# Tile 0 of a mixture-of-experts layer takes its experts by id, and a part of the weight conversion changes engine and order

## What is computed

```python
# layer 1, one head of 256
q, k = rope(bf16(x @ Wq.T)), rope(bf16(x @ Wk.T))
o = where(causal, exp(q @ k.T / 16), 0).sum(-1)        # one number per row
x1 = layernorm(x + relu(o * fc1_w + fc1_b) @ fc2_w.T + fc2_b)
# layer 2, 12 experts, three routers, the best 3 of 12 of each
C1, C2, C3 = (top3_softmax(x1 @ P_w.T @ U.T) for U in (U1, U2, U3))   # zero elsewhere
h = gelu(sum_e C1[:, e] * (x1 @ W1[e].T))
y = sum_e C2[:, e] * (h @ W2[e].T) + C3 @ b2
out = layernorm(x1 + y)
```

## Time and profile before

| | us |
|---|---|
| median of 3 runs | 280.23 |
| lowest, highest | 279.22, 280.51 |
| the profiled execution | 280.48 |
| its span, first to last instruction | 278.7 |

### The profile page before, as it was taken

One profiled execution on the slowest core, in us unless ns is written; L12 is line 12 of the kernel. 1 busy time (PEld: TensorE's weight loads), 2 busy tenths in 40 slices (PEclk: granted clock), 3 DMA queues, 4 the chain that ended last, 5 costly groups with the idle time before them and its releaser, 6 DMA issues.

```text
span 278.7 us, 6485 instructions
## 1 busy us (share of the span) xinstructions
PE 257.4 (92%) x2016; PEld 191.4 (69%) x2016; DVE 213.2 (77%) x668; ACT 173.9 (62%) x376; POOL 180.2 (65%) x367
## 2 busy tenths in 40 slices
PE   7999999998989985998999999999999999899980
PEld 5445444554436773877789798799798798798960
DVE  0359959859969865688998899899897788766671
ACT  2235975765852730675958957967878858656541
POOL 2640004999989899747885775775775864856551
PEclk9999999999999996899999999999999999999996
DMA  7999994996000000000010101001011010111012
GB/s 226 378 397 372 164 221 72 220 151 84 0 1 2 0 4 0 0 5 17 13 31 22 34 24 39 22 20 42 19 26 35 20 40 19 33 32 38 23 36 61
DMA packets 19546, 20.51 MB, mean 74 GB/s; under 512 B 1643, under 2 KB 18870, under 8 KB 18998
## 3 DMA queue, kind: packets, MB, share of 16 engines
q1 hardware_dynamic: 18518, 19.14, 27.9%
q10 hardware_dynamic: 992, 0.93, 1.2%
HBM read 15.78 MB, written 4.19 MB: 72 GB/s over the span
## 4 chain that ended last, share of the span: by engine, by line
PE 37%; POOL 21%; SPq 16%; ACT 12%; issue 6%; DVE 5%; DMA 1%; POOLq 0%; ACTq 0%; DVEq 0%
PE bank L1117 31%; POOL W L471 7%; POOL wtmp L468 5%; POOL W L470 5%; SPq L371 4%; SPq L376 3%; ACT L705 3%; SPq L393 2%; SPq L380 2%; DVE early L1535 2%; ACT early L726 2%; PE bank L1197 2%; ACT L788 2%; SPq L404 1%; PE bank L995 1%
## 5 line engine op out<-in xcount | busy, mean ns | idle before, releaser
L1117 PE MATMUL bank<-W,early 128*128 (+1 forms) x630 | 77.7, 278 | 6.0 <-DVE early L1535 3.7
L1117 PE MATMUL bank<-W,x1T 128*128 (+1 forms) x630 | 75.9, 273 | 0.5 <-ACT early L837 0.5
L1117 PEld LDWEIGHTS bank<-W,early 128*128 128x128 f16 x630 | 61.9, 100 | 15.8 <-issue 4.2
L1117 PEld LDWEIGHTS bank<-W,x1T 128*128 128x128 f16 x630 | 60.9, 98 | 8.6 <-issue 1.1
L920 PE MATMUL bank<-early,wqk 128*128 128x512 f32 x128 | 60.1, 602 | 1.1 <-DMA early<-in_xT 1.1
L1535 DVE SCALAR_TENSOR_TENSOR early<-bank,Csel,early 128x256 f32<-128x256 f32 x95 | 45.7, 481 | 9.2 <-PE bank L1117 2.7
L591 POOL TENSOR_TENSOR early<-early 128x256 f32<-128x256 f32 x29 | 21.0, 725 | 28.4 <-DVE early L1535 27.1
L920 PEld LDWEIGHTS bank<-early,wqk 128*128 128x128 f32 x128 | 22.4, 190 | 21.8 <-issue 21.2
L661 ACT ACTIVATE qk<-bank 128x512 bf16<-128x512 f32 x32 | 19.0, 595 | 29.1 <-PE bank L920 28.9
L788 ACT ACTIVATE early<-early 128x256 f32<-128x256 f32 x32 | 13.3, 417 | 35.5 <-DVE early L1535 35.4
L1289 DVE TENSOR_TENSOR xturn<-qk,turn 128x2048 bf16<-128x2048 bf16 x16 | 20.4, 1276 | 15.7 <-ACT qk L661 15.7
(11 more groups left out here) (139 smaller groups left out, 451.6 us busy)
## 6 DMA issues: line engine op xcount, KB each, us to landing
early<-in_xT SPq DMA_DIRECT2D x16, 256.0 KB, 7.8
xs<-in_x SPq DMA_DIRECT2D x32, 128.0 KB, 6.8
out<-early SPq DMA_DIRECT2D x32, 128.0 KB
W<-in_w1T SPq DMA_DIRECT2D x1, 2048.0 KB, 12.2
W<-in_w2T SPq DMA_DIRECT2D x1, 2048.0 KB, 12.8
W<-in_w1T SPq DMA_DIRECT2D x1, 1024.0 KB, 7.7
W<-in_w2T SPq DMA_DIRECT2D x1, 1024.0 KB, 14.3
wqk<-in_wqkT ACTq DMA_DIRECT2D x1, 512.0 KB, 3.8
```

The source lines that it names most:

```text
L1117: mm = pe.matmul(where[:, 0:DIM], lhs(hx, c), w, start=(k == 0), stop=(k == 5))
```

## The change

Tile 0 takes three experts by id in both mixtures, as all other tiles do (`experts_of` and `dense_expert` go). All of W2 must then be converted before `second(0)`. Of W2, six experts (5 down to 0) are now on ScalarE and VectorE and six on GpSimd; W1 stays at four and eight. GpSimd's order is written anew: three pieces, `norm_scale(0)`, two pieces, `norm_scale(1)`, three pieces (W1 is complete), the softmax weights, `select_of(0)`, `C3_split(0)`, five pieces of W2, `bias_add(0, 0)`, the sixth. `route_count(0)` moves ahead of `project(7, 2)`. Group 0's mask is made as the other groups' is, with 4 strikes in place of 12. On TensorE the order after the chunks is: first mixtures of tiles 0, 1, 2, 3, then the second ones of 0 and 1.

```diff
-NB = 4
+NB = (4, 6)
+HERE, THERE = NB[0], NE - NB[0]
...
+            seconds = () if i < GT else (0, 1, 2) if i == GT else (i - 2,)
+            order = [(t, 1, j) for t in seconds for j in range(TOPK)]
+            order += [(i, 0, j) for j in range(TOPK)] if i < NT else []
...
+        def here(n):
+            return (0, NB[0] - 1 - n) if n < HERE else (1, NB[1] - 1 - (n - HERE))
+        def there(n):
+            return (0, NB[0] + n) if n < THERE else (1, NB[1] + n - THERE)
...
             def w_piece(n):
-                m, e = n // (NE - NB), NB + n % (NE - NB)
+                m, e = there(n)
...
-                t = slice(max(GT * g, 1), GT * (g + 1))
+                t = slice(GT * g, GT * (g + 1))
...
-            piece = 0
-            for c in range(NCH):
-                for j in range(4):
-                    if (c, j) == (NCH - 1, 1):
-                        continue
-                    if (c, j) == (3, 3):
-                        norm_scale(0)
-                    if (c, j) == (5, 1):
-                        norm_scale(1)
-                    if (c, j) == (6, 1):
-                        chosen_exps(0)
-                        weights_of(0)
-                    if (c, j) == (6, 2):
-                        C3_split(0)
-                        select_of(0)
-                    if c >= 4:
-                        w_piece(piece)
-                        piece += 1
-            bias_add(0, 0)
-            w_piece(piece)
+            for n in range(THERE):
+                if n == 3:
+                    norm_scale(0)
+                if n == 5:
+                    norm_scale(1)
+                w_piece(n)
+            chosen_exps(0)
+            weights_of(0)
+            select_of(0)
+            C3_split(0)
+            for n in range(THERE, 2 * NE - sum(NB)):
+                if n == 2 * NE - sum(NB) - 1:
+                    bias_add(0, 0)
+                w_piece(n)
...
             norm_scale(2)
+            bias_add(0, 1)
             gate_parts(2)
-            bias_add(0, 1)
+            chosen_exps(1)
             row_scale(0)
-            chosen_exps(1)
...
# ScalarE, after the chunks
             begin(0)
+            begin(1)
             exps(NCH - 1, 0)
-            w_high(NB + 2)
+            w_high(HERE + 2)
             exps(NCH - 1, 1)
-            w_high(NB + 3)
+            w_high(HERE + 3)
+            C3T_copy(0)
             gelu(0)
-            C3T_copy(0)
-            begin(1)
+            gelu(1)
+            begin(2)
+            w_high(HERE + 4)
+            bias_copy(0, 0)
             h_high(0)
-            bias_copy(0, 0)
-            gelu(1)
+            gelu(2)
+            w_high(HERE + 5)
+            begin(3)
+            h_high(1)
+            bias_copy(0, 1)
+            gelu(3)
             normed(2, 0)
-            bias_copy(0, 1)
+            exp_route(1)
             x1_high(2, 0)
-            exp_route(1)
             normed(2, 1)
-            h_high(1)
-            begin(2)
-            gelu(2)
-            gate_copy(2)
             final(0)
             h_high(2)
             x1_high(2, 1)
-            begin(3)
-            gelu(3)
+            gate_copy(2)
...
# TensorE, after the chunks
+            load_ids(0)
+            x1_transpose(1, 1)
+            pe.wait_ge(exp_done, SPC * (NCH - 1))
+            pe.wait_ge(w_split, THERE)
+            pe.wait_ge(wlo_done, HERE)
+            routed_first(0, range(0, 2))
+            pe.wait_ge(qk_copied, 4 * NCH)
+            routed_first(0, range(2, TOPK))
+            fc(2, 0)
+            routed_first(1, range(0, 2))
+            pe.wait_ge(gate_copied, 4)
+            scores(NCH - 1, 0)
+            routed_first(1, range(2, TOPK))
+            fc(2, 1)
+            scores(NCH - 1, 1)
             C3_transpose(0)
-            routed_first(1)
+            routed_first(2)
             pe.wait_ge(exp_done, SPC * NCH)
             h_transpose(0)
             bias(0, 0)
             route_logits(1)
+            h_transpose(1)
+            routed_first(3)
             bias(0, 1)
+            pe.wait_ge(wlo_done, sum(NB))
+            pe.wait_ge(w_split, 2 * NE - sum(NB))
+            second(0, range(TOPK))
             x1_transpose(2, 0)
             fc(3, 0)
+            second(1, range(TOPK))
             h_transpose(2)
             x1_transpose(2, 1)
+            route_count(1)
+            fc(3, 1)
+            gate_transpose(2)
             fc(4, 0)
...
# VectorE, after the chunks (w_low(HERE) is in chunk 7)
+            first_mixture(0)
             fc_add(2, 0)
             x1_low(1, 1)
+            w_low(HERE + 1)
+            first_mixture(1)
             fc_add(2, 1)
+            w_low(HERE + 2)
             norm_stats(2)
+            w_low(HERE + 3)
+            first_mixture(2)
             h_low(0)
+            w_low(HERE + 4)
             route_max(1)
+            w_low(HERE + 5)
+            first_mixture(3)
+            h_low(1)
+            second_mixture(0)
+            x1_low(2, 0)
             route_strike(1)
+            route_mask(1)
             row_stats(0)
             fc_add(3, 0)
+            second_mixture(1)
             route_sums(1)
             row_stats(1)
             h_low(2)
             x1_low(2, 1)
+            route_ids(1)
+            fc_add(3, 1)
+            norm_stats(3)
             fc_add(4, 0)
```

The masks of group 0 and its count, VectorE and TensorE:

```diff
-                tiles = range(1 if g == 0 else 0, GT)
-                for t in tiles:
+                for t in range(GT):
                     mm = pe.matmul(bank[MISC][0:1, Z:Z + NM * NE], const(C_ONES, 1),
                                    mask[:, NR * t:NR * t + NM, :].rearrange("p g e -> p (g e)"),
-                                   start=(t == tiles[0]), stop=(t == GT - 1))
+                                   start=(t == 0), stop=(t == GT - 1))
...
-                    if g == 0 or n % NR == NM:
+                    if n % NR == NM:
                         mr = dve.match_replace(zrest[:, n, :], top8[:, n, :], zs[:, n, :], -NO_LOGIT)
```

More of the change, by code:

```diff
@@ L358, in later @@
             return 2 <= g < NG
-        PARTS = (slice(0, NB), slice(NB + 2, NB + 6), slice(NB + 6, WS))
-        HALVES = [slice(p.start + 2 * n, p.start + 2 * n + 2) for p in PARTS for n in range(2)]
+        PARTS = (slice(0, NB[0]), slice(NB[0] + 2, NB[0] + 6), slice(NB[0] + 6, WS))
+        HALVES = [slice(e + 2 * (e >= NB[1]), e + 2 * (e >= NB[1]) + 2) for e in range(0, NE, 2)]
         block = ctx.enter_context(nc.Block())
@@ L694, in w_high @@
             def w_high(n):
-                m, e = n // NB, NB - 1 - n % NB
+                m, e = here(n)
                 act.wait_ge(scale_done, 1)
-                if n % NB:
+                if n not in (0, HERE):
                     act.wait_ge(wlo_done, n)
@@ L776, in begin @@
                 n = slot[t, 0, 0]
-                if t == 0:
-                    act.wait_ge(C_done, 1)
-                elif t % GT == 0 or t == 1:
+                if t % GT == 0:
                     act.wait_ge(csel_done, t // GT + 1)
                 act.wait_ge(slot_done, n + 1)
-                c0 = C[:, 0, 0, 1:2] if t == 0 else Csel[:, t, 0, 0:1]
-                act.activation(acc1[:, t % 2, :], bank[place[n]][:, 0:DIM], ACT.Copy, scale=c0).then_inc(acc_begun, 1)
+                wait(act, gelu_done, t - 1)
+                act.activation(acc1[:, t % 2, :], bank[place[n]][:, 0:DIM], ACT.Copy, scale=Csel[:, t, 0, 0:1])\
+                    .then_inc(acc_begun, 1)
             def gelu(t):
@@ L823, in _ @@
                     x1_high(1, 0)
-                    w_high(NB)
+                    w_high(HERE)
                 if c == NCH - 1:
-                    w_high(NB + 1)
+                    w_high(HERE + 1)
             def h_high(t):
@@ L1126, in mixture @@
                         pe.wait_ge(acc_begun if act else slot_added, count)
-                    e = dense_expert(m, j) + 1 if t == 0 else held_ids[t // GT][REC * m + j]
-                    products(bank[place[n]], lhs, m, e).then_inc(slot_done, 1)
+                    products(bank[place[n]], lhs, m, held_ids[t // GT][REC * m + j]).then_inc(slot_done, 1)
             def load_ids(g):
@@ L1156, in _ @@
                     scores(c - 1, 0)
+                if c == NCH - 1:
+                    route_count(0)
                 project(c, 2)
                 early_aux(c, 2, early)
-                if c == NCH - 1:
-                    route_count(0)
                 if c:
@@ L1171, in _ @@
                     gate_spread(c - 1)
[L1173 to L1190, removed]
-            first(range(8, NE))
             def h_transpose(t):
@@ L1212, in _ @@
             route_logits(1)
-            pe.wait_ge(wlo_done, NM * NB - 1)
-            second(0, range(0, NB - 1))
-            pe.wait_ge(wlo_done, NM * NB)
-            second(0, range(NB - 1, NB))
-            pe.wait_ge(w_split, NM * (NE - NB) - 2)
-            second(0, range(NB, NB + 2))
+            h_transpose(1)
+            routed_first(3)
             bias(0, 1)
```

(36 more changed lines are left out.)

51 lines of the change are left out of this document (8 added, 43 removed).

## The result

The median is 1280.9 us (1280.04 to 1286.02, four runs) against 280.37 us before: a ratio of 4.575, 95% interval 4.557 to 4.594. The forecast was 1240, with a range of 1010 to 1660. The profiled execution has a span of 1278.2 us.

What follows compares the result with a forecast made beforehand. TensorE was taken to bound the kernel, with waits on GpSimd's queue; the change adds a dense second pass. 280.5 + 1.2 + 2 + 224 + 630 + 102 = 1240 us, range 1010 to 1660.

Steps and rivals of the forecast that it cites:

- The branch: Behind `over`: counting tile 0 makes `over` nonzero, so the whole second layer is done again, densely; chance 0.95.
- Rival 1: Branch behind `over` not taken, only the first pass counts: 281.7 us, or 278.0 if GpSimd's queue ceases to bind; chance 0.05.
- Rebuilding C: VectorE's loop remaking the weights C in the repetition: 640 steps at 0.35 us, 224 us (bounds 109 to 339).
- The dense products: Repetition's 768 products, each summed by VectorE after waits at computed values: 0.82 us each, 630 us (499 to 1052).
- Between the mixtures: Repetition, per tile: gelu, transposes, h_high and h_low come alone, 3.2 us x 32 = 102 us (80 to 130).
- The sum: Total of all terms, today's time plus first pass, start, rebuild, products and gaps: 1240 us (bounds 966 to 1808).
- the first pass: Everything ahead of the repetition: removed products and delayed GpSimd work nearly balance, +1.2 us (-4 to +5).
- the start: Entering the repetition: waits for the last store and six id loads, 2 us.
- Rival 2: TensorE at the lower clock sets the second pass's pace, 1.3 us a product: 369 us more, 1610; chance 0.20.
- The router's weights and select: GpSimd's steps between its W1 pieces and the W2 pieces in the first pass: 6 us.
- The six pieces behind it: GpSimd's last W2 pieces: 13.7 + 0.5 us for five, 1.3 for the bias, 2.6 for the sixth, ending at 115.0.
- The late norm_scale(0): GpSimd's norm_scale(0) behind three pieces delays ScalarE's normed(0, 0) to 59 us; TensorE leaves the projections at 96.5.

Runs made afterwards that it cites:

- run 3: Kernel before the change, with only route_count(0) edited to count tile 0 too; tile 0 stays dense: 1283.23 us, ratio 4.573.
- run 1: Changed kernel with route_count(0) counting tiles 1 to 3 only; tile 0 still takes three experts by id: 285.08 us, ratio 1.020.
- run 6: Changed kernel with three more sem_inc on VectorE ahead of each repetition sum that follows another sum: 1472.8 us.
- run 7: Changed kernel with TensorE multiplying zeros (20 and 12 matmuls) ahead of its two waits between the repetition's mixtures: 1230.4 us.
- run 2: Changed kernel with tile 0 not counted and norm_scale(0) put back ahead of GpSimd's first piece: 274.36 us, ratio 0.978.
- run 4: Kernel before the change, with only norm_scale(0) moved behind three pieces of weights on GpSimd: 290.6 us, ratio 1.036.
- run 5: Changed kernel with four matmuls instead of six in each product of the repetition: 1251.5 us.
- run 9: Kernel before, with six experts of W2 on ScalarE and VectorE, two pieces less on GpSimd, bias ahead of the last: 276.19 us, ratio 0.987.
- run 8: Kernel before the change, with GpSimd's bias_add(0, 0) one piece of weights earlier, nothing left out: 280.05 us, ratio 0.9997.

## Why the prediction was right, and where its terms were off

- **The branch.** Right: `over` is decided by data, one tile in 32 decides it, and the edit that counts it is enough, alone, to bring 1003 us in the kernel before (run 3) and to take 996 us away in the changed one (run 1). Rival 1 is out.
- **Rebuilding C.** 224 forecast, 224.4 measured. The hit to 0.2% is luck: the bounds, 0.17 and 0.53 us a step, were far apart, and I took their middle, 0.35. The measured mean is 0.35.
- **The dense products.** The mechanism was right (VectorE with its waits at computed values, not TensorE), the term mis-sized: 0.725 us each, not 0.82. I had charged six register instructions at 0.12 and 0.17 for the link, 0.89 us in all, and let all but 0.34 of it hide behind the sum before. That was my estimate, and no run shows it; what is left to see between two sums is 0.24 us, and three increments more between them were not hidden (run 6: 1.004 us a sum).
- **Between the mixtures.** Mis-sized the other way: 6.7 us per tile instead of 3.2. One part is the sum's own slip. The 3.9 us run from the end of a sum, a pace of 0.82 from start to start, so the row gave 3.9 + 0.48 - 0.82 = 3.6 and not 3.2. Two things were not in the sum. At a tile's end VectorE does the statistics before it can go on with the next tile: 1.2 us on the mean. And TensorE starts each second mixture at the lower clock (0.50 to 0.59 behind the first sum, in all 32), so three sums there come late, 1.2 us in all, and the passage is 4.2 instead of 3.75 us; run 7 shows both go with the clock, 50.5 / 32 = 1.6 us per tile.
- **The sum.** The two errors of the dense part, -73 and +113 us, partly cancel and leave +40, which is nearly all of 1280 - 1240. That the forecast came this near is luck in these two terms; the first pass and the start, +3.0 and -2.8, cancel too.
- **Rival 2** named a real thing. The clock does drop in every tile, to 0.50 (the second sum of each second mixture is 1.2 us behind the first, with 0.73 in run 7), but from 3 us behind the start of the first sum on it is 1.00 again, in all 32, and it is 0.89 on the mean of the dense part. Since TensorE does not set the pace of most sums, a seventh of the price arrives, 50.5 of 369 us (run 7).
- **The first pass.** The places up to 91 us were right: normed(0, 0) at 59.27 (59 said), TensorE's restarts at 60.4 and 62.2 (60 and 62.0), GpSimd's wait until 77.40 (77.9), the router's weights from 90.90 (91.0 by the same sum). The terms that were off come behind it. The router's weights and select were put at 6 us and took 7.6 (90.90 to 98.50). In the kernel before the same operations take 6.3. VectorE's rotations (92.36 to 94.33 and 95.94 to 98.03) now ran beside five of them. Three of these took longer than before: 1.46 us at 92.32 instead of 0.35 (at 83.62 us there), 1.14 at 96.31 instead of 0.28, 0.64 at 97.51 instead of 0.26; one, at 93.74, took 0.72 instead of 1.35. That the rotations are the cause is read from the two timelines, not tested. The six pieces behind it took 0.8 us more than said. So the last piece ended at 117.40, not 115.0, and fc(4, 0) came at 130.98, not 128.1. The late norm_scale(0) was to bring TensorE out of the projections at 96.5, 12.5 us late; it was 95.11, 11.1 late. With all else equal it costs 10.7 us at the end (runs 1 and 2), 10.2 in the kernel before (run 4).

## What to carry to other kernels

Before costing the instructions of a change, ask which branches of the program depend on data and whether the edit moves what they test: here a single line of a count was worth 996 us, and all the rest of the change 4.7. In this loop on the chip it counted how many instructions stand behind the wait of the engine that carries the chain, and not which engine has the most arithmetic: TensorE was busy for 609 of the 772 us and VectorE, which set the pace, for 407; a third of TensorE's matmuls was worth 29 us (run 5), three increments per sum on VectorE 192 (run 6). And when a wait at the end of an in-order queue is removed, look at what stands next in the same queue: shortening the queue gave 1.3% (run 9), moving one item in it alone nothing (run 8).

## What had not been expected of the hardware

A `sem_inc` on VectorE that waits for nothing cost 0.093 us (run 6: a third of 1.004 - 0.725). Two dependent sums, with two waits at computed values and two `sem_inc` between them, lie 0.24 us apart; the earlier trace rows have 0.15 where the values are plain. And the loop that rebuilds C took 224.4 us in one program and 231.5 in another that differs only ahead of it; in the second a wait of up to 0.5 us ahead of one and the same step appeared in 30 of its turns:

```profile
DVE dz L1659 <- DVE zrest L1658: 7.8, 30, 0.5
```

(engine, line, waited for: us in total, times, longest; VectorE's waits from 283 to 500 us in run 3). The changed kernel has no such entry. This step makes some 3.6 of the 7 us; the other 3.4 are at the turn of the loop, 0.64 us from its last operation to the next copy instead of 0.53. No run shows the cause.
